# A batch-conditioned linear layer on one core: ring bursts in pairs, one part of the weights loaded twice, and other load times

## The chip, the cores and the metric

The kernel runs on one core of one Trainium2 chip. Its time is device time in microseconds, the median of several executions; the profile is of one execution.

## The reference

```python
masked_w = weight * mask[None, :, :]                 # (8, 512, 512)
w_bot = jnp.einsum('bg,got->bot', y, masked_w)       # y: (128, 8), one 512x512 matrix per batch row
return x + (jnp.einsum('bnt,bot->bno', x, w_bot) + bias)   # x: (128, 128, 512), fp32
```

So each of 128 batch rows has its own matrix, a mix of eight masked ones, and the kernel adds an identity to it so that x itself comes out of the same product.

## The kernel before

**Units, groups, steps.** The work is cut into 16 units: 4 blocks of 32 batch rows times 4 slices of 128 outputs. A unit has 8 groups of 4 batch rows. A step n (0 to 127) is one group: `group(n)` (L529) makes 16 fp32 products of 128x128 (32 passes in the trace, L543) into one of two PSUM banks; VectorE adds the bias (`add_bias`, L458), ScalarE issues the store of the output (`store_out`, L392). Its matrices lie in the buffer `wbot`, which holds one unit.

**Bursts.** The matrices of a unit are made while the unit before is used, in 8 bursts of 4 chunks; a chunk fills one of six PSUM banks (`ps1`). Bursts 0 to 15 are fp32 products (`first_burst`, L506), evicted by VectorE (L445) and completed with an identity by GpSimd (`add_one`, L357). From burst 16 on (`burst`, L524) a chunk is 8 bf16 products of 98 rows by 64 columns, evicted by ScalarE (`evict`, L387) into `wbot`. Chunk k of burst c takes the place of batch row 4c + k of the unit that was used last, so its eviction waits until group c has come to that batch row (`chunk_ready`). `bursts_before(n)` says which bursts TensorE makes ahead of group n: one each step, burst n + 8. A chunk also waits for room, that is for the eviction of the chunk six before it (`room`).

**The ring.** A burst's stationary rows stand in one of six slots: 6 blocks of 16 rows (the mask times weights in three bf16 parts, part 1 three times, part 2 twice, part 3 once) and two rows of an identity. SyncE loads parts 1 and 2 (32 rows, 256 KB), part 3 (128 KB) and the identity rows (16 KB); VectorE copies within the slot, 32 rows (`duplicate`, L436) and 16 rows (L437). A load waits until the burst six before has been made, and until the parts that it reads have been stored.

**The parts.** Each weight is read and used from its three parts. They are made in 32 tiles: load (`raw`, L242), mask multiply on VectorE (L430), first part by a cast on ScalarE (L378), remainder on GpSimd (L348), second part on ScalarE (L382), third on GpSimd (L350), store to `w_parts` in memory (`store_parts`, L255), which are then loaded again for each unit. `TILES_AT` says at which step a tile is made: 0 to 3 during the first bursts, 4 to 15 in steps 0 to 7, from step 8 on two tiles in three steps, the last at step 30.

**The order.** All is written out by hand. SyncE issues every load and the parts' stores, in the order of its program: at step n the stores of the tiles of step n - 2, a load of raw weights, ring loads (`load_burst`), and a load of x (`load_x`, L284, 1 MB, one of 8 slots) where `X_AT` says so. It waits in that order too. x is read four times 8 loads, each load used by one group of four units; the loads of the second 8 go out at steps 25, 26, 28, 29, 31, 33, 34, 36, for use from step 32 to 39.

## Time and profile before

| | us |
|---|---|
| median of 3 runs | 663.26 (662.29 to 663.32) |
| the profiled execution | 660.4 |
| its span, first to last instruction | 658.6 |
| TensorE busy (matmul) | 633.7, 96% |
| VectorE busy | 452.4, 69% |
| ScalarE busy | 312.3, 47% |
| GpSimd busy | 123.2, 19% |
| DMA | 141.30 MB, mean 215 GB/s |

The span and what lies around it make the 660.4 us. A share is an average over the span: GpSimd works only in the first third, with the tiles, and DMA is at its busiest there.

### The profile page before, as it was taken

To read this page: it belongs to the slowest core of one execution; us is meant where nothing else is said; L and a number is where in the kernel's file an instruction comes from. 1 tells how busy PE (TensorE), PEld (TensorE's weight loads), DVE (VectorE), ACT (ScalarE), POOL (GpSimd) and SP (SyncE) were. 2 spreads that over 40 slices of the span, in tenths; PEclk is the share of its full clock that TensorE was granted. 3 is DMA by queue.
4 is the path that set the end of the run, shared out by engine and by line. 5 is a ranking of instruction groups with operands and counts; after the bars stand their busy time and mean duration, and the time that the engine had idled before them with its cause. 6 is when DMAs were issued, how large, how long until landed. Compare 5 with 4: busy or idle time off the path is not lost.

```text
span 658.6 us, 18464 instructions
## 1 busy us (share of the span) xinstructions
PE 633.7 (96%) x7808; PEld 598.7 (91%) x7808; DVE 452.4 (69%) x449; ACT 312.3 (47%) x513; POOL 123.2 (19%) x95
## 2 busy tenths in 40 slices
PE   6989979999999997999999999999999999999998
PEld 2467759999999997999999999999999999999997
DVE  4976769889999763767666676766767667676521
ACT  0132216666666553555555555555555555555500
POOL 5685746445555000000000000000000000000000
PEclk9999999999999997999999999999999999999999
DMA  8979939889889995565569986555579995553122
GB/s 321 388 228 311 370 80 289 244 229 246 238 266 335 272 304 161 144 161 140 150 206 278 282 291 198 150 141 159 137 214 284 280 314 158 159 146 99 53 78 80
DMA packets 62881, 141.30 MB, mean 215 GB/s; under 512 B 7694, under 2 KB 33392, under 8 KB 52976
## 3 DMA queue, kind: packets, MB, share of 16 engines
q1 hardware_dynamic: 43856, 106.19, 54.5%
q10 hardware_dynamic: 18944, 33.93, 16.1%
q8 instruction: 62, 1.02, 0.6%
q14 instruction: 19, 0.16, 0.1%
HBM read 93.96 MB, written 46.14 MB: 213 GB/s over the span
## 4 chain that ended last, share of the span: by engine, by line
PE 81%; DVE 10%; DMA 3%; issue 3%; POOL 2%; ACT 0%; SPq 0%; DVEq 0%; ACTq 0%
PE ps L543 61%; PE ps L524 13%; PE ps L506 7%; DVE ring L437 5%; DVE ring L436 3%; DMA xs<-in_x 3%; DVE staged L458 1%; DVE raw L430 1%; POOL wbot L357 1%; DMA first_sb<-in_first 1%; POOL raw L348 1%; POOL parts L350 0%; DVE yblk L464 0%; ACT parts L378 0%; ACT wbot L387 0%
## 5 line engine op out<-in xcount | busy, mean ns | idle before, releaser
L543 PE MATMUL ps<-wbot,xs 128*128 128x128 f32 x4096 | 489.9, 278 | 7.8 <-DMA xs<-in_x 5.6
L543 PEld LDWEIGHTS ps<-wbot,xs 128*128 128x128 f32 x4096 | 471.1, 193 | 12.3 <-issue 6.4
L387 ACT ACTIVATE wbot<-ps 128x512 f32<-128x512 f32 x448 | 275.0, 614 | 237.6 <-PE ps L543 237.0
L458 DVE TENSOR_TENSOR staged<-ps,bias_sb 128x512 f32<-128x512 f32 x128 | 88.4, 691 | 176.9 <-PE ps L543 176.6
L437 DVE COPY ring<-ring 16x4096 bf16<-16x4096 bf16 x112 | 151.0, 1348 | 3.5
L436 DVE COPY ring<-ring 32x4096 bf16<-32x4096 bf16 x112 | 136.4, 1218 | 3.5
L524 PE MATMUL ps<-ydiag,ring 98*128 98x64 bf16 x3584 | 123.1, 193 | 8.2 <-DVE ring L437 8.2
L524 PEld LDWEIGHTS ps<-ydiag,ring 98*128 98x128 bf16 x3584 | 119.8, 98 | 10.9 <-issue 9.7
L348 POOL TENSOR_TENSOR raw<-raw,parts 128x512 f32<-128x512 f32 x32 | 49.3, 1540 | 70.4 <-ACT parts L378 70.4
L445 DVE TENSOR_TENSOR wbot<-ps,ring 128x512 f32<-128x512 f32 x64 | 43.4, 688 | 14.4 <-PE ps L506 10.0
L350 POOL TENSOR_TENSOR parts<-raw 128x512 bf16<-128x512 f32 x32 | 48.8, 1524 | 2.5
L378 ACT ACTIVATE parts<-raw 128x512 bf16<-128x512 f32 x32 | 19.9, 624 | 56.6 <-DVE raw L430 44.3
L430 DVE TENSOR_TENSOR raw<-raw,mask_sb 128x512 f32<-128x512 f32 x32 | 34.5, 1087 | 0.5
L506 PE MATMUL ps<-yblk,xs 128*128 128x512 f32 x64 | 29.2, 618 | 5.6 <-DVE yblk L464 5.6
L506 PEld LDWEIGHTS ps<-yblk,xs 128*128 128x128 f32 x64 | 12.7, 200 | 21.3 <-issue 15.0
L506 PE MATMUL ps<-yblk,ring 128*128 128x512 f32 x64 | 28.6, 592 | 0.0
L382 ACT ACTIVATE parts<-raw 128x512 bf16<-128x512 bf16 x32 | 19.9, 622 | 17.9 <-POOL raw L348 10.2
L506 PEld LDWEIGHTS ps<-yblk,ring 128*128 128x128 f32 x64 | 11.6, 190 | 12.0 <-issue 12.0
L357 POOL TENSOR_TENSOR wbot<-wbot,first_sb 128x512 f32<-128x512 f32 x16 | 20.2, 1266 | 11.1 <-DVE wbot L445 11.0
L464 DVE TENSOR_TENSOR yblk<-first_sb 128x512 f32<-128x512 f32 x1 | 0.7, 693 | 4.9 <-DMA first_sb<-in_first 4.9
L378 ACT ACT_TABLE_LOAD x1 | 1.3, 1283 | 2.7 <-issue 2.7
L338 POOL TENSOR_SCALAR staged<-staged,pick_sb 98x128 bf16<-98x128 bf16 x3 | 1.8, 602 | 0.3
(10 smaller groups left out, 4.0 us busy)
## 6 DMA issues: line engine op xcount, KB each, us to landing
xs<-in_x SPq DMA_DIRECT2D x32, 1024.0 KB, 10.0
out<-staged ACTq DMA_DIRECT2D x128, 256.0 KB, 3.3
ring<-w_parts SPq DMA_DIRECT2D x112, 256.0 KB, 4.0
ring<-w_parts SPq DMA_DIRECT2D x112, 128.0 KB, 4.3
w_parts<-parts SPq DMA_DIRECT2D x32, 384.0 KB, 5.9
raw<-in_w SPq DMA_DIRECT2D x16, 512.0 KB, 8.8
ring<-in_w SPq DMA_DIRECT2D x4, 512.0 KB, 15.2
ring<-in_eye SPq DMA_DIRECT2D x112, 16.0 KB
```

The costliest lines, as they stand in the source:

```text
L348: eng.tensor_tensor(at, at, w1, ALU.subtract).then_inc(s_rest, 1)
L350: eng.tensor_tensor(parts[:, t % PARTN, 2, :, :], at, high_half(t), ALU.subtract).then_inc(s_p3, 1)
L357: eng.tensor_tensor(at, at, ident_sb[:, c * CO:(c + 1) * CO].unsqueeze(1).to_broadcast([P, W, CO]), ALU.add).then_inc(s_diag, 1)
L387: eng.activation(chunk_place(b, k), chunk_sums(b, k), ACT.Copy).then_inc(s_ev_a, 1)
L430: eng.tensor_tensor(at, at, mask_sb[:, h % 2, :].unsqueeze(1).to_broadcast([P, TG, TW]), ALU.mult).then_inc(s_mul, 1)
L436: eng.tensor_copy(ring[2 * ROWS:4 * ROWS, i, :], ring[0:2 * ROWS, i, :]).then_inc(s_dup, 1)
L437: eng.tensor_copy(ring[4 * ROWS:5 * ROWS, i, :], ring[0:ROWS, i, :]).then_inc(s_dup, 1)
L445: eng.tensor_tensor(at, ps1[(b * KT + k) % S1B][:, :].rearrange("p (b o) -> p b o", o=CO), mask_t_sb[:, k, o:o + CO].unsqueeze(1).to_broad ...
L458: eng.tensor_tensor(staged[:, n % OUTB, :].rearrange("p (b o) -> p b o", b=GB), ps2[n % S2B][:, :].rearrange("p (b o) -> p b o", b=GB), bi ...
L506: ins = eng.matmul(ps1[(b * KT + k) % S1B][:, :], raw01_sb[u][:, c, k * P:(k + 1) * P], yblk[:, :], start=True, stop=True)
L524: ins = eng.matmul(ps1[at % S1B][:, g * W * OJ:(g + 1) * W * OJ], ring[0:KALL, i, k * CW + g * P:k * CW + (g + 1) * P], ydiag[:, first:fir ...
L543: ins = eng.matmul(ps2[n % S2B][:, b * SL:(b + 1) * SL], xs[:, load % GROUPS * GB + b, k, :], at, start=(k == 0), stop=(k == KT - 1))
```

## The change

Five parts. (1) `bursts_before`: from step 8 on, bursts are made before groups 0, 2, 4, 6 and 7 of a unit: one, two, two, two, one. (2) The slots' order is another, the first three ring loads go out at step 2, burst 16's copy is made at step 6, and the other copies one step ahead as before, from step 8 on. (3) Bursts 16 to 39 load part 1 a second time (16 rows, 128 KB, with a semaphore of its own), and VectorE copies only the 32 rows. (4) Tiles from 16 on come at seven steps for five, x at ten steps for eight loads; in a step SyncE's stores stand behind its loads, and a ring load goes out only if the tiles that it reads were made three steps ago. (5) At the start GpSimd's subtractions of tiles 0 and 1 stand behind the identity additions 4 and 5, those of 2 and 3 behind all eight.

```diff
-            **{8 + (t - 16) * 3 // 2: (t,) for t in range(16, TILES)}}
+            **{8 + (t - 16) * 7 // 5: (t,) for t in range(16, TILES)}}
 def bursts_before(n):
     if n < GROUPS:
         return ((), (8,), (9,), (10,), (11,), (12,), (13,), (14, 15))[n]
-    return (n + GROUPS,) if n + GROUPS < BURSTS else ()
+    if n + GROUPS >= BURSTS or n % GROUPS in (1, 3, 5):
+        return ()
+    return (n + GROUPS,) if n % GROUPS in (0, GROUPS - 1) else (n + GROUPS - 1, n + GROUPS)
-X_AT = {_g: LAST_USE[_g - _g % GROUPS - GROUPS] + 1 + _g % GROUPS * 8 // 5 for _g in range(GROUPS, XLOADS)}
+X_AT = {_g: LAST_USE[_g - _g % GROUPS - GROUPS] + 1 + _g % GROUPS * 9 // 7 for _g in range(GROUPS, XLOADS)}
 def slot_of(b):
-    return (b - FB + 4) % RING
+    return (4, 5, 0, 2, 3, 1)[(b - FB) % RING]
+def thrice(b):
+    return b < FB + 3 * CS
 def free_before(b):
     r = b - FB
     if r < 3:
         return 0
+    if r == RING - 1:
+        return GROUPS
...
+COPIES = [0] * (FB + 1)
+for _b in range(FB, BURSTS):
+    COPIES.append(COPIES[-1] + (1 if thrice(_b) else 2))
 SyncE, load_burst
-                elif b >= FB + 4:
+                elif b >= FB + 5:
+                    eng.wait_ge(s_ev_v, FB * KT)
+                elif b >= FB + 3:
                     eng.wait_ge(s_s1, FB * KT)
-                elif b >= FB + 3:
-                    eng.wait_ge(s_ev_v, FB * KT)
...
+                if thrice(b):
+                    w1 = scratch[h, 0, :, :, c % KT * BW:(c % KT + 1) * BW].rearrange("g o c -> (g o) c")
+                    eng.dma_start(ring[4 * ROWS:5 * ROWS, i, :], w1).then_inc(s_w1[i], 16)
 SyncE, the steps
-            kept = EARLY
+            kept = 0
             for n in range(STEPS):
-                for t in TILES_AT.get(n - 2, ()):
-                    store_parts(t)
-                    kept = t + 1
+                kept = max((kept, EARLY if n >= 2 else 0, *(t + 1 for t in TILES_AT.get(n - 3, ()))))
...
                 for g in range(GROUPS, XLOADS):
                     if X_AT[g] == n:
                         load_x(g)
+                for t in TILES_AT.get(n - 2, ()):
+                    store_parts(t)
 GpSimd
             for c in range(CS):
                 add_one(c)
-                if c >= CS - EARLY:
-                    subtract(c - CS + EARLY)
+                if c in (4, 5):
+                    subtract(c - 4)
+            subtract(2)
+            subtract(3)
 VectorE
-                eng.tensor_copy(ring[4 * ROWS:5 * ROWS, i, :], ring[0:ROWS, i, :]).then_inc(s_dup, 1)
+                if not thrice(b):
+                    eng.tensor_copy(ring[4 * ROWS:5 * ROWS, i, :], ring[0:ROWS, i, :]).then_inc(s_dup, 1)
...
-                while made < BURSTS and made <= LAST_BURST[min(n + 1 + AHEAD, STEPS)]:
+                if n == GROUPS - 2:
+                    duplicate(FB)
+                    made += 1
+                while n >= GROUPS and made < BURSTS and made <= n + GROUPS + AHEAD:
                     duplicate(made)
                     made += 1
 TensorE, burst
+                if thrice(b):
+                    eng.wait_ge(s_w1[i], 16 * (turn + 1))
                 eng.wait_ge(s_eye[i], 16 * (turn + 1))
-                eng.wait_ge(s_dup, 2 * (b - FB + 1))
+                eng.wait_ge(s_dup, COPIES[b + 1])
```

TensorE's program from group 8 to group 10, before; a row `ps_k<-ydiag,ring` is one chunk of a burst and its PSUM bank, a row `<-wbot,xs` a group:

```order
L543 MATMUL ps_0<-wbot,xs 128x128 x16
L524 MATMUL ps_2<-ydiag,ring 128x64 x8
L524 MATMUL ps_3<-ydiag,ring 128x64 x8
L524 MATMUL ps_4<-ydiag,ring 128x64 x8
L524 MATMUL ps_5<-ydiag,ring 128x64 x8
L543 MATMUL ps_1<-wbot,xs 128x128 x16
L524 MATMUL ps_0<-ydiag,ring 128x64 x8
L524 MATMUL ps_1<-ydiag,ring 128x64 x8
L524 MATMUL ps_2<-ydiag,ring 128x64 x8
L524 MATMUL ps_3<-ydiag,ring 128x64 x8
L543 MATMUL ps_0<-wbot,xs 128x128 x16
```

The same place after:

```order
L568 MATMUL ps_0<-wbot,xs 128x128 x16
L568 MATMUL ps_1<-wbot,xs 128x128 x16
L549 MATMUL ps_2<-ydiag,ring 128x64 x8
L549 MATMUL ps_3<-ydiag,ring 128x64 x8
L549 MATMUL ps_4<-ydiag,ring 128x64 x8
L549 MATMUL ps_5<-ydiag,ring 128x64 x8
L549 MATMUL ps_0<-ydiag,ring 128x64 x8
L549 MATMUL ps_1<-ydiag,ring 128x64 x8
L549 MATMUL ps_2<-ydiag,ring 128x64 x8
L549 MATMUL ps_3<-ydiag,ring 128x64 x8
L568 MATMUL ps_0<-wbot,xs 128x128 x16
```

Bursts 17 and 18 stand in a row, and their last two chunks use the banks of their first two.

VectorE's program at steps 7 and 8, before: evictions of burst 15 (`wbot<-ps`), the ring copies of burst 16, a mask multiply, a bias add (`staged<-ps`):

```order
L445 TENSOR_TENSOR wbot<-ps_0,ring 128x512
L445 TENSOR_TENSOR wbot<-ps_1,ring 128x512
L445 TENSOR_TENSOR wbot<-ps_2,ring 128x512
L445 TENSOR_TENSOR wbot<-ps_3,ring 128x512
L436 COPY ring<-ring 32x4096
L437 COPY ring<-ring 16x4096
L430 TENSOR_TENSOR raw<-raw,mask_sb 128x512
L458 TENSOR_TENSOR staged<-ps_1,bias_sb 128x512
```

After, from the copy of burst 16 on:

```order
L455 COPY ring<-ring 32x4096
L449 TENSOR_TENSOR raw<-raw,mask_sb 128x512 x2
L478 TENSOR_TENSOR staged<-ps_0,bias_sb 128x512
L465 TENSOR_TENSOR wbot<-ps_2,ring 128x512
L465 TENSOR_TENSOR wbot<-ps_3,ring 128x512
L465 TENSOR_TENSOR wbot<-ps_4,ring 128x512
L465 TENSOR_TENSOR wbot<-ps_5,ring 128x512
L465 TENSOR_TENSOR wbot<-ps_0,ring 128x512
L465 TENSOR_TENSOR wbot<-ps_1,ring 128x512
L465 TENSOR_TENSOR wbot<-ps_2,ring 128x512
L465 TENSOR_TENSOR wbot<-ps_3,ring 128x512
L449 TENSOR_TENSOR raw<-raw,mask_sb 128x512
```

The copy of burst 16, now one of 32 rows alone, has moved ahead of the eight evictions of step 7.

SyncE's program at steps 29 to 32, before, with the semaphores that a row waits for (`s_store` tells that a tile's parts are in memory, `s_s2` that groups are done, `s_s1` that bursts are made):

```order
L284 DMA xs<-in_x 128x2048 [waits s_s2]
L255 DMA w_parts<-parts 128x6x256 [waits s_p3,s_p2]
L284 DMA xs<-in_x 128x2048 [waits s_s2]
L255 DMA w_parts<-parts 128x6x256 [waits s_p3,s_p2]
L272 DMA ring<-in_eye 2x2048 [waits s_store1,s_store0,s_s1,s_store4,s_store3]
L275 DMA ring<-w_parts 32x4096
L276 DMA ring<-w_parts 16x4096
```

After, steps 28 to 32:

```order
L301 DMA xs<-in_x 128x2048 [waits s_s2]
L269 DMA w_parts<-parts 128x6x256 [waits s_p3,s_p2] x2
L286 DMA ring<-in_eye 2x2048 [waits s_store2,s_store1,s_s1,s_store0,s_store4]
L289 DMA ring<-w_parts 32x4096
L290 DMA ring<-w_parts 16x4096
L301 DMA xs<-in_x 128x2048 [waits s_s2] x2
L269 DMA w_parts<-parts 128x6x256 [waits s_p3,s_p2]
L286 DMA ring<-in_eye 2x2048 [waits s_store1,s_store0,s_s1,s_store4,s_store3]
L289 DMA ring<-w_parts 32x4096
L290 DMA ring<-w_parts 16x4096
```

The loads of x come one to two steps sooner by then, and the ring load that waits for the last tiles still stands behind the last store.

## Rows read from the trace of the kernel before

**Rows 1.** The page: an engine's busy time; two groups (count | busy, mean ns)

```profile
PE 633.7 (96%) x7808; PEld 598.7 (91%) x7808; DVE 452.4 (69%) x449; ACT 312.3 (47%) x513; POOL 123.2 (19%) x95
...
L543 PE MATMUL ps<-wbot,xs 128*128 128x128 f32 x4096 | 489.9, 278 | 7.8 <-DMA xs<-in_x 5.6
...
L524 PE MATMUL ps<-ydiag,ring 98*128 98x64 bf16 x3584 | 123.1, 193 | 8.2 <-DVE ring L437 8.2
```

**Rows 2.** What TensorE waited for: us in total, times, longest us

```profile
PE ps L524 <- DVE ring L437: 8.2, 9, 3.5
...
PE ps L543 <- DMA xs<-in_x: 5.6, 2, 4.4
```

**Rows 3.** Windows: us, busy of PE, PEld, DVE, ACT, POOL, clock, DMA share, GB/s

```profile
194.00:220.00 26.00, 24.88 (x360) 24.51 (x360) 22.60 (x21) 16.98 (x29) 12.36 (x7) 1.00 1.04 335
...
110.00:180.00 70.00, 67.00 (x917) 66.08 (x916) 63.00 (x54) 44.98 (x77) 36.27 (x20) 1.00 0.87 243
```

**Rows 4.** The chain of waits, a steady step: start us, us, what

```profile
442.77 0.94 PE ps L524 x32
443.70 3.65 PE ps L543 x32
```

**Rows 5.** Timeline at step 8: start us, us, instruction [idle before <-releaser]

```profile
92.14 1.15 POOL L357 TENSOR_TENSOR wbot<-wbot,first_sb 128x512 f32<-128x512 f32 x1 [4.93 <-DVE wbot L445]
...
93.15 0.69 DVE L445 TENSOR_TENSOR wbot<-ps,ring 128x512 f32<-128x512 f32 x1 [0.20 <-PE ps L543]
...
96.59 1.30 PE L524 MATMUL ps<-ydiag,ring 98*128 98x64 bf16 x32 [3.55 <-DVE ring L437]
```

**Rows 6.** Windows of the groups behind the two long waits

```profile
253.30:259.24 5.94, 5.94 (x38) 5.93 (x39) 0.00 (x0) 1.81 (x3) 0.00 (x0) 0.63 0.21 79
97.70:102.95 5.25, 5.25 (x42) 5.24 (x40) 4.69 (x3) 1.86 (x4) 4.02 (x2) 0.71 1.03 239
```

**Rows 7.** Timeline of a steady step

```profile
448.13 3.82 PE L543 MATMUL ps<-wbot,xs 128*128 128x128 f32 x32
...
449.36 0.62 ACT L387 ACTIVATE wbot<-ps 128x512 f32<-128x512 f32 x1 [1.29 <-PE ps L543]
```

**Rows 8.** Timeline of a step with tiles

```profile
109.11 1.22 DVE L436 COPY ring<-ring 32x4096 bf16<-32x4096 bf16 x1
110.36 2.07 DVE L437 COPY ring<-ring 16x4096 bf16<-16x4096 bf16 x1
...
112.78 1.09 PE L524 MATMUL ps<-ydiag,ring 98*128 98x64 bf16 x32 [0.65 <-DVE ring L437]
```

**Rows 9.** What SyncE's queue waited for: us in total, times, longest

```profile
SPq L204 <- DMA w_parts<-parts: 11.4, 2, 5.8
```

**Rows 10.** DMA from 180.9 to 253.3 us

```profile
DMA packets 9297, 21.15 MB, mean 292 GB/s; under 512 B 960, under 2 KB 5568, under 8 KB 7534
```

**Rows 11.** Timeline ahead of group 0

```profile
35.01 1.60 POOL L357 TENSOR_TENSOR wbot<-wbot,first_sb 128x512 f32<-128x512 f32 x1
...
35.53 1.27 DVE L445 TENSOR_TENSOR wbot<-ps,ring 128x512 f32<-128x512 f32 x2
...
36.76 1.46 PE L543 MATMUL ps<-wbot,xs 128*128 128x128 f32 x11 [1.95 <-POOL wbot L357]
```

**Rows 12.** The chain of waits, the last unit, which has no bursts

```profile
627.02 0.14 issue
627.16 28.17 PE ps L543 x250
```

**Rows 13.** Timeline: two evictions of ScalarE in a row

```profile
483.55 1.25 ACT L387 ACTIVATE wbot<-ps 128x512 f32<-128x512 f32 x2 [0.57 <-PE ps L543]
```

**Rows 14.** Timeline: ScalarE, an eviction and a cast

```profile
132.10 0.62 ACT L387 ACTIVATE wbot<-ps 128x512 f32<-128x512 f32 x1 [0.28 <-PE ps L543]
132.61 0.62 ACT L378 ACTIVATE parts<-raw 128x512 bf16<-128x512 f32 x1
```

**Rows 15.** Timeline: GpSimd's subtraction

```profile
138.43 1.98 POOL L348 TENSOR_TENSOR raw<-raw,parts 128x512 f32<-128x512 f32 x1 [1.44 <-ACT parts L378]
```

More of the change, by code:

```diff
@@ L185, in cond_resid_kernel @@
         s_w3 = [sem(f"s_w3_{i}") for i in range(RING)]
+        s_w1 = [sem(f"s_w1_{i}") for i in range(RING)]
         s_eye = [sem(f"s_eye{i}") for i in range(RING)]
```

## The prediction

> **What bounds the kernel now.** I read the page's engine line, then the list of what TensorE waited for, then the windows, and only then the timelines of the places which those three name. TensorE is busy for 633.7 of 658.6 us [rows 1], so anything off its path counts only by the TensorE waits that it makes or ends. Those waits are few [rows 2]: 8.2 us for VectorE's copies in the ring (9 waits, the longest 3.5), 5.6 us for two loads of x, 1.9 us for GpSimd at the first group; the 5.6 us for yblk are the start and stay. The windows say where: DMA is 0.87 busy from 110 to 180 us, with the clock granted at 1.00, and saturated from 194 to 220 us (share 1.04, 335 GB/s) [rows 3]. Away from the waits a step is 0.94 us of burst plus 3.65 us of group, 4.59 us [rows 4].
>
> **Part 1, the copy ahead of the first ring burst: -5.2 us.** Before, VectorE makes burst 16's two copies behind the last eviction of unit 1, so TensorE stands for 3.55 us [rows 5]. Its clock is then granted at 0.71 over the next group, which takes 5.25 us where one at full clock takes 3.82, and the burst takes 1.30 for 1.09 [rows 5 to 8]: 1.6 us. After, the copy stands one step earlier, and slots 4, 5, 0 are loaded at step 2, long before. What is late next: VectorE's eviction ends at 93.84 us (93.15 + 0.69) and GpSimd's identity add at 93.29 (92.14 + 1.15) [rows 5]; TensorE's group ends at 93.0 (96.59 - 3.55) and the burst covers it up to 93.0 + 0.94 = 93.9. So both terms go whole: 3.55 + 1.6 = 5.2.
>
> **Part 2, part 1 of the weights loaded twice: -4.7 us.** The other eight copy waits (8.2 - 3.5) lie in the steps with tiles: VectorE copies for 1.22 us and then for 2.07 us beside GpSimd, and TensorE's group has ended 0.65 us before [rows 8]. The 16-partition copy goes for bursts 16 to 39, that is for all those steps; 2.07 (or 1.22) us less on VectorE is more than the 0.65 by which it was late, in each of the eight places. 4.7 us go. The price is 24 transfers of 128 KB. Bytes per step rise from about 1.11 MB (ring 0.41, store 0.39 and raw 0.26 at 2 tiles in 3 steps, out 0.26) to 1.3 MB (ring 0.54, tiles 5 in 7 steps), at 4.6 us 280 GB/s, against 292 over the longest saturated stretch and 335 in a shorter one [rows 3, 10]. A ring load has 3 to 5 steps (14 us and more) before its copy, so some lag is covered. I take 0; if the queue moved only 250 GB/s, it would lag by 16 steps x 0.6 = 10 us, still within the cover, and that is the other end for the ring; it would be paid at x (rival b).
>
> **Part 3, x over ten groups, loads behind their stores: -6.9 us.** Before, x costs 5.6 us of waits [rows 2], and the group behind the second runs at clock 0.63, 5.94 us for 3.82 [rows 6, 7]: 7.7 in all. Two causes show: SyncE stands twice, 11.4 us together, at a ring load which waits for a store issued just before [rows 9], and 21.15 MB had to move from 180.9 us, where the first load of x goes out, to 253.3, where the last has landed, at 292 GB/s [rows 10]. After, up to the last x load the queue holds 8 loads of x (8.4 MB), 10 ring loads (4.1) and one more w1, 5 stores (2.0), a raw load (0.5) and 13 outputs (3.4): 18.6 MB, 63.7 us at 292. It has 14 steps (25 to 39) of about 4.68 us, 65.5 us. The slack is under 2 us, and one SyncE wait remains (the load for burst 44 stands right behind the last store). I leave 0.8 us of wait as a mean: 7.7 - 0.8 = 6.9. Ends: all 7.7 gone, or all still there.
>
> The Trainium skill (DMA: Bandwidth & Descriptors, Bandwidth) gives 341 GB/s for a 1 MB transfer by itself; by that the 18.6 MB would take 55 us, no wait could remain and the sum would be 0.8 us lower. The row of 292 GB/s over 72 us, with small and large transfers mixed, decides against counting on it.
>
> **Part 4, GpSimd's order at the start: -0.8 us.** Group 0 waits until GpSimd's last identity add ends at 36.61 us [rows 11], behind two subtractions of tile 2. Without these (2.2 us) it would end near 34.4, while TensorE waits from 34.8 (36.76 - 1.95). But VectorE's last eviction ends at 36.80 (35.53 + 1.27) and group 0 needs it 0.7 us in, so only some 0.5 us is open, plus what VectorE gains with less of GpSimd beside it. Ends 0 and 1.95; I take 0.8.
>
> **Part 5, bursts in pairs: +9.6 us, and this decides the size.** What goes: a group after a burst takes 3.65 us, eight groups in a row take 28.17 us for 250 matmuls, less 0.28 of latency 3.57 for 32 [rows 1, 4, 12]. So a switch costs 0.08 us; three fewer in each of 14 units are 42 x 0.08 = 3.4 us. What comes: a pair writes eight PSUM banks and there are six, so its seventh and eighth chunks wait for the evictions of its first and second. Before, two groups' worth of time lay between. With 0.94/32 us a matmul, the first chunk's last matmul starts 0.20 us into the pair; it takes 0.19, and ScalarE starts about 0.10 later (449.36 against 448.13 + 0.08 + 7 x 0.112 + 0.28 = 449.27 in the steady step [rows 1, 7]): 0.49. Two evictions in a row take 1.25 us [rows 13]: 1.74. TensorE starts 0.14 us after a ScalarE release [rows 12]: 1.88. The eighth chunk would start at 56 matmuls, 1.64. That is 0.24 us of wait in every pair, 42 x 0.24 = 10.1 us. The seventh is free: 0.49 + 0.61 + 0.14 = 1.24 before 1.40. Bounds: ScalarE starts a cast 0.51 us behind an eviction [rows 14]; were evictions to follow each other so, the wait would be 0.13 (5.5 us in all); at the distance that a group's batches now give them, 8 x 28.17/250 = 0.90 [rows 12], it is 0.52 (21.8 us). I take the row of two evictions in a row.
>
> In the tile steps ScalarE also has casts. Behind an even step's last eviction (about 6.0 us into the pair) come two casts at 0.51; GpSimd's subtraction takes up to 1.98 us [rows 15] from 7.7 on, that tile's second cast runs at 9.6, and where the odd step has a tile too, its cast at 10.1, so the next pair's first eviction starts at 10.6 instead of 9.85. 0.16 us of that is slack: about 0.65 us for the four pairs at steps 10, 14, 18 and 28, and 0.1 for three others, 2.9 us. Ends 0 and 4.
>
> Part 5 in all: -3.4 + 10.1 + 2.9 = +9.6.
>
> **Sum.** -5.2 - 4.7 - 6.9 - 0.8 + 9.6 = -8.0 us on the profiled execution: span 658.6 to 650.6, its time 660.4 to 652.4. The median of the runs is 663.26, 2.9 above the profiled one; I forecast a median of 655.3.
>
> **Rivals.** (a) The pairs do not wait, since evictions follow at less than I think or the matmul stream is slower at the switch. For it: the wait is a small difference of two times. Against it: even at 0.51 the eighth chunk is 0.13 late. Then 655.3 - 10.1 - 2.9 = 642.3 us. (b) The x wait stays, because 128 KB more per burst and a faster pace fill the queue that is already at 1.04: 655.3 + 6.9 = 662.2 us. For it: under 2 us of slack by my own count. Against it: of SyncE's two stands one is left. (c) The slower side: ScalarE's evictions in a pair follow each other at 0.90 instead of 0.62 us. Place: the eighth chunk of each of the 42 pairs. Price 21.8 instead of 10.1: 655.3 + 11.7 = 667.0 us. It decides from a wait of (10.1 + 8.0)/42 = 0.43 us a pair on. Against it: the 1.25 us row. (d) The short waits lower the clock: each pair would then be followed by a group at 5.9 instead of 3.8 us, 42 x 2.1 = 88 us, 743 us. Against it: copy waits like the one of 0.65 us lie in the window 110 to 180, clock 1.00 [rows 3, 8]. The Trainium skill (TensorE: Matmul & The Clock Gate, A second HAM failure mode) has such a case, TensorE idling briefly between groups as it cycles through PSUM banks; this trace does not agree, with 1.00 there.
>
> **How the numbers follow.** Forecast 0.62, (a) 0.17, (b) 0.12, (c) 0.08, (d) 0.01. The forecast's own range, from its bounds (pairs 5.5 to 14, tiles 0 to 4, x up to 3), is 649 to 660. To hold 8 in 10 I reach a good part towards (a) and take in (b): 645 to 663. 0.2% (1.3 us) is what a measurement of this kernel can tell from no change, so faster means below 661.9: all of (a), nearly all of the forecast and a part of (b), 0.86; same 0.06; slower, (c) with the rest of (b), 0.08.
>
> **What would show it.** Part 1: TensorE goes from group 7 into burst 16 with no idle time and the clock stays at 1.0. Part 2: no TensorE wait on a ring copy from 100 to 215 us. Part 3: no wait on x at groups 38 and 39, SyncE waiting once for a store. Part 5: 42 new TensorE waits on ScalarE's eviction, in each pair's last chunk, 0.13 to 0.3 us each, longer in the tile steps; a unit of eight steps takes 36.5 + 0.7 = 37.2 us where it took 36.7. It would be wrong if a unit takes 36.5 us or less, if those waits are over 0.4 us, or if bursts wait for ring loads.

## The result, and the profile after

The changed kernel takes 644.84 us (median of 4 runs, 643.54 to 649.15) against 662.77 us for the kernel before (4 runs, 661.58 to 663.32): ratio 0.9743, 95% interval 0.9694 to 0.9792. On another chip it was 645.95 against 661.52, ratio 0.9755 (0.9727 to 0.9783). The forecast was 655.3 us with a range from 645 to 663; the direction was right, the gain more than twice as large (17.9 us for 8.0), and the time just outside the range. The profiled execution took 643.54 us, its span 641.1. A unit of eight steps (groups 40 to 47) takes 36.46 us where it took 36.71: at 36.5 or less the prediction had said that it would be wrong.

The page of the changed kernel, which answers to [rows 1]:

```profile
PE 629.0 (98%) x7808; PEld 594.3 (93%) x7808; DVE 411.7 (64%) x425; ACT 297.0 (46%) x513; POOL 110.2 (17%) x95
...
L568 PE MATMUL ps<-wbot,xs 128*128 128x128 f32 x4096 | 478.2, 277 | 0.8 <-DVE wbot L465 0.4
...
L549 PE MATMUL ps<-ydiag,ring 98*128 98x64 bf16 x3584 | 117.2, 193 | 2.8 <-DVE ring L457 2.5
```

TensorE does the same work; its idle time before groups fell from 7.8 to 0.8 us and before bursts from 8.2 to 2.8. What it waited for, beside [rows 2], again us in total, times, longest; the 5.2 us for yblk at the start are left out:

```profile
PE ps L549 <- DVE ring L457: 2.5, 1, 2.5
PE ps L568 <- DVE wbot L465: 0.4, 1, 0.4
PE ps L568 <- ACT wbot L406: 0.2, 1, 0.2
PE ps L568 <- POOL wbot L374: 0.2, 1, 0.2
```

All eight waits of the tile steps, the one ahead of burst 16 and both waits on x are gone. One new wait of 2.5 us has come, and there is no list of 42 waits on ScalarE. That list alone does not settle it: in the run with five banks below every pair takes 0.48 us longer, and TensorE's list there names two such waits, 0.6 us in all. What settles it is the length of a pair. The windows of [rows 3], in the changed kernel:

```profile
110.00:180.00 70.00, 69.87 (x996) 69.52 (x996) 41.32 (x41) 47.56 (x84) 29.23 (x22) 1.00 1.02 310
194.00:220.00 26.00, 26.00 (x358) 25.97 (x355) 14.65 (x15) 14.16 (x25) 2.30 (x2) 1.00 0.90 288
```

DMA is now full in the tile steps (1.02 where it was 0.87), and VectorE is busy for 41.3 of 70 us where it was for 63.0.

A steady pair in the chain of waits (start us, us, what), beside [rows 4]:

```profile
443.81 1.87 PE ps L549 x64
```

64 matmuls in 1.87 us are two bursts of 0.94 with nothing between; so are all 30 pairs from group 40 on (1.87 or 1.88). The timeline shows ScalarE beside it, an eviction 0.44 us after the pair's first matmul and the next one 0.51 later:

```profile
443.64 2.03 PE L549 MATMUL ps<-ydiag,ring 98*128 98x64 bf16 x64
...
444.08 0.62 ACT L406 ACTIVATE wbot<-ps 128x512 f32<-128x512 f32 x1 [3.13 <-PE ps L549]
...
444.59 1.58 ACT L406 ACTIVATE wbot<-ps 128x512 f32<-128x512 f32 x3
```

I cut both kernels into stretches, from the first matmul of one group to that of another (us, from the timelines; one burst of 0.94 us that stood ahead of group 9 before stands behind its start after):

| stretch | before | after | difference |
|---|---|---|---|
| start to group 1 | 43.84 | 43.71 | -0.1 |
| group 1 to 9 | 59.89 | 53.63 | -6.3 |
| group 9 to 32 | 111.47 | 106.91 | -4.6 |
| group 32 to 40 | 44.81 | 40.71 | -4.1 |
| group 40 to 120 | 366.13 | 363.73 | -2.4 |
| group 120 to the end | 32.44 | 32.44 | 0 |

The differences add up to the 17.5 us between the spans. Corrected for the moved burst, the second and third rows are -5.3 and -5.5.

The one long wait that is left, in the chain of the changed kernel:

```profile
203.77 0.44 SPq L301
...
204.31 13.15 DMA w_parts<-parts
...
217.91 3.47 DMA ring<-w_parts
...
221.40 0.04 DVE ring L455
...
222.65 1.23 DVE ring L457
...
224.13 1.09 PE ps L549 x32
```

The last store of parts is issued behind two loads of x (L301) into a busy queue (DMA 0.94 busy from 164 to 217 us) and takes 13.15 us to land. SyncE stands for it at the ring load of burst 44; that load takes 3.47 us, two copies follow, and TensorE has been idle for 2.46 us. Then the clock is granted at half for a while: groups 36 and 37 take 8.86 us together where two take 7.23. (The texts on record call this the stop at group 35; it stands between groups 35 and 36.) The window behind the stop, in the columns of [rows 3]:

```profile
225.30:228.60 3.30, 3.30 (x17) 3.30 (x17) 2.10 (x2) 1.49 (x3) 0.00 (x0) 0.50 0.99 300
```

The stop also hides something. The last load of x lands at 239.58 us, and group 39, which needs it, starts at 240.37. The stop and its clock had put that group back by 4.25 us; without them it would have been due at 236.1, and would have waited some 3.4 us for x.

### The profile page after: what moved, and what is told of

The parts are those of the page before. It is cut to its first block, busy times and chain, and to the rows that moved or that the text cites. A ratio compares the mean times of both kernels' runs of the same rounds, so it can differ in the third digit from the quotient of the medians.

```text
span 641.1 us, 18487 instructions
## 1 busy us (share of the span) xinstructions
PE 629.0 (98%) x7808; PEld 594.3 (93%) x7808; DVE 411.7 (64%) x425; ACT 297.0 (46%) x513; POOL 110.2 (17%) x95
## 3 DMA queue, kind: packets, MB, share of 16 engines
q8 instruction: 62, 1.02, 0.7%
## 4 chain that ended last, share of the span: by engine, by line
PE 93%; DMA 3%; DVE 2%; issue 1%; ACT 1%; SPq 0%; ACTq 0%; DVEq 0%
PE ps L568 70%; PE ps L549 15%; PE ps L529 7%; DMA w_parts<-parts 2%; DVE wbot L465 1%; DVE raw L449 1%; ACT wbot L406 1%; DMA first_sb<-in_first 1%; DMA ring<-w_parts 1%; DVE ring L457 0%; DVE yblk L484 0%; DVE staged L478 0%; SPq L301 0%; SPq L286 0%; DVE ring L455 0%
## 5 line engine op out<-in xcount | busy, mean ns | idle before, releaser
L568 PE MATMUL ps<-wbot,xs 128*128 128x128 f32 x4096 | 478.2, 277 | 0.8 <-DVE wbot L465 0.4
L568 PEld LDWEIGHTS ps<-wbot,xs 128*128 128x128 f32 x4096 | 466.0, 193 | 5.5 <-issue 4.7
L406 ACT ACTIVATE wbot<-ps 128x512 f32<-128x512 f32 x448 | 259.5, 610 | 224.2 <-PE ps L568 115.8
L549 PE MATMUL ps<-ydiag,ring 98*128 98x64 bf16 x3584 | 117.2, 193 | 2.8 <-DVE ring L457 2.5
L549 PEld LDWEIGHTS ps<-ydiag,ring 98*128 98x128 bf16 x3584 | 114.8, 98 | 4.3 <-issue 2.6
L457 DVE COPY ring<-ring 16x4096 bf16<-16x4096 bf16 x88 | 107.2, 1218 | 2.7
L365 POOL TENSOR_TENSOR raw<-raw,parts 128x512 f32<-128x512 f32 x32 | 45.7, 1428 | 68.9 <-ACT parts L397 68.8
L367 POOL TENSOR_TENSOR parts<-raw 128x512 bf16<-128x512 f32 x32 | 39.1, 1221 | 2.5
L449 DVE TENSOR_TENSOR raw<-raw,mask_sb 128x512 f32<-128x512 f32 x32 | 36.6, 1155 | 0.5
```

Source lines behind the costliest of these rows:

```text
L365: eng.tensor_tensor(at, at, w1, ALU.subtract).then_inc(s_rest, 1)
L367: eng.tensor_tensor(parts[:, t % PARTN, 2, :, :], at, high_half(t), ALU.subtract).then_inc(s_p3, 1)
L406: eng.activation(chunk_place(b, k), chunk_sums(b, k), ACT.Copy).then_inc(s_ev_a, 1)
L449: eng.tensor_tensor(at, at, mask_sb[:, h % 2, :].unsqueeze(1).to_broadcast([P, TG, TW]), ALU.mult).then_inc(s_mul, 1)
L457: eng.tensor_copy(ring[4 * ROWS:5 * ROWS, i, :], ring[0:ROWS, i, :]).then_inc(s_dup, 1)
L549: ins = eng.matmul(ps1[at % S1B][:, g * W * OJ:(g + 1) * W * OJ], ring[0:KALL, i, k * CW + g * P:k * CW + (g + 1) * P], ydiag[:, first:fir ...
```

## The experiments

Each set of runs has runs of the kernel before on the same chip; ratios are to those, with 95% intervals. A run that is compared with the changed kernel across two chips is compared by these ratios. Stretches are of the profiled execution, in the order group 9 to 32, 32 to 40, 40 to 120; the changed kernel has 106.91, 40.71, 363.73, the kernel before 111.47, 44.81, 366.13.

**Are the pairs free?** One burst before each group, all else as changed:

```diff
-    if n + GROUPS >= BURSTS or n % GROUPS in (1, 3, 5):
-        return ()
-    return (n + GROUPS,) if n % GROUPS in (0, GROUPS - 1) else (n + GROUPS - 1, n + GROUPS)
+    return (n + GROUPS,) if n + GROUPS < BURSTS else ()
```

> The changed kernel with one burst before each group again, all else as changed. Theory S (a pair saves three switches of 0.08 us a unit and waits for nothing outside the tile steps): from group 40 to group 120 the time goes back from 363.7 to 366.1 us, as in the kernel before, and from group 9 to 32 the 1.0 us of pair waits goes while 8 switches (0.6 us) come back; whole kernel 2 to 4 us slower than the changed one if the stop at group 35 stays alike, ratio about 1.005. Theory P (the pairs do wait, as the prediction had it, and something else in the change made up for it): one burst a step would be faster than the changed kernel by up to 10 us. The stop of 2.5 us behind the ring load of burst 44 should shrink or stay, since burst 44 is needed at step 36 in both.

Measured: 649.52 us, ratio 0.9831 (0.9800 to 0.9862); stretches 105.53, 44.98, 366.13. The last is the kernel before's to the hundredth: in 10 units, 30 pairs save 2.40 us, 0.08 us each, and wait for nothing. The first shows the copies' part without the pairs: 105.53 against the kernel before's 111.47, 5.9 us for the same 23 bursts. In the tile steps the pairs cost instead: 105.53 is 23 plain steps, and the changed kernel, less its one burst more, takes 0.4 us longer, in spite of 8 switches saved. The stop at burst 44 grew to 5.6 us, with half clock behind it; that is the greater part of the difference between the two kernels (4.3 of 6.4 us of span), and why it came out above the 2 to 4 us expected. Whether one burst a step made the stop grow is not shown; it differs between executions of one kernel too, as below.

**What is a bank short worth?** Five banks instead of six:

```diff
-S1B = 6
+S1B = 5
```

> The changed kernel with five PSUM banks for bursts instead of six, so that a pair's sixth, seventh and eighth chunk wait for the evictions of its first, second and third. With the times that the changed kernel's trace shows (first eviction starts 0.44 us into the pair, the next ones 0.51 apart, each 0.61 long, TensorE about 0.05 behind): the sixth chunk is free (1.10 before 1.17), the seventh waits 0.20 (1.61 against 1.41), the eighth 0.25 more (2.10 against 1.85): 0.45 us a pair, 42 pairs, 19 us slower than the changed kernel, about 664 us. With the prediction's constants (0.49, 0.62, 0.14 behind) it would be 0.07 + 0.40 + 0.39 = 0.86 us a pair, 36 us slower, about 681 us. If pairs are not tied to evictions at all: no change.

Measured: 661.08 us, ratio 1.0024 (0.9989 to 1.0060); stretches 111.25, 38.14, 378.07. The last is 14.34 us more over 30 pairs, 0.48 each, where the constants of the changed kernel's trace gave 0.45 and the prediction's 0.86. The middle one is shorter than the changed kernel's: the profiled execution, in which burst 44 is due 4 us later, has no stop there. A pair, in its timeline:

```profile
442.81 2.50 PE L549 MATMUL ps<-ydiag,ring 98*128 98x64 bf16 x64
...
443.25 0.61 ACT L406 ACTIVATE wbot<-ps 128x512 f32<-128x512 f32 x1 [3.13 <-PE ps L549]
...
443.76 1.58 ACT L406 ACTIVATE wbot<-ps 128x512 f32<-128x512 f32 x3
...
444.41 0.29 PEld L549 LDWEIGHTS ps<-ydiag,ring 98*128 98x128 bf16 x8 [0.15 <-ACT wbot L406]
...
444.90 0.29 PEld L549 LDWEIGHTS ps<-ydiag,ring 98*128 98x128 bf16 x8 [0.20 <-ACT wbot L406]
```

The second eviction ends near 443.76 + 0.61 = 444.37, and TensorE loads weights at 444.41: it follows a release by 0.04 us. So the mechanism of the prediction is real, and with six banks it just fails to bite.

Its weight loads' waits for ScalarE, two in each pair (us in total, times, longest), and its clock:

```profile
PEld ps L549 <- ACT wbot L406: 16.0, 83, 0.5
```

```profile
core 0: 656.5 us, clock 1.000
```

In this execution 83 waits, 0.2 us as a mean and none over 0.5, did not lower the clock once; of the other nine runs five had 0.994 to 0.997, and no trace says what lowered it there. The Trainium skill (TensorE: Matmul & The Clock Gate, A second HAM failure mode) tells of a kernel whose TensorE idles briefly and often between groups as it cycles through PSUM banks, and whose clock falls and rises with it; in this run, with two short waits in each pair, it does not fall.

**Pairs alone on the kernel before:** the edit of the first experiment the other way, and nothing else of the change.

```diff
-    return (n + GROUPS,) if n + GROUPS < BURSTS else ()
+    if n + GROUPS >= BURSTS or n % GROUPS in (1, 3, 5):
+        return ()
+    return (n + GROUPS,) if n % GROUPS in (0, GROUPS - 1) else (n + GROUPS - 1, n + GROUPS)
```

> The kernel before with bursts in pairs alone, all else as before. Theory S: outside the tile steps 3.4 us less by 42 switches. In the tile steps VectorE makes two bursts' copies in a row (2 x (1.22 + 2.07 or 1.22)) behind one bias add, and each pair waits for them: the copies of a pair, 5 to 6.6 us, stand in one step of 4.6 with the mask multiply, so its eight waits of 0.65 us stay or grow. Sum between 5 us faster and 5 us slower than before, 100 to 660 us apart: from group 40 to 120 363.7 us instead of 366.1. Theory P: 42 x 0.24 = 10 us slower there.

Measured: 748.7 us, ratio 1.1333 (1.1298 to 1.1369); stretches 152.16, 41.36, 415.89. I had not seen this: 49.8 us more than the kernel before over 30 pairs, 1.66 each as a mean; two spells of half clock, 1.6 us each, are in it. VectorE and TensorE in the steady part:

```profile
435.49 1.22 DVE L438 COPY ring<-ring 32x4096 bf16<-32x4096 bf16 x1
436.74 1.22 DVE L439 COPY ring<-ring 16x4096 bf16<-16x4096 bf16 x1
437.99 1.22 DVE L438 COPY ring<-ring 32x4096 bf16<-32x4096 bf16 x1
439.24 1.22 DVE L439 COPY ring<-ring 16x4096 bf16<-16x4096 bf16 x1
```

```profile
440.71 1.09 PE L526 MATMUL ps<-ydiag,ring 98*128 98x64 bf16 x32 [1.40 <-DVE ring L439]
```

The old rule makes both bursts' copies in the step before the pair, four in a row, and the second burst starts only when the fourth has ended at 440.46. The changed rule (`made <= n + GROUPS + AHEAD`) makes one burst's copies in each step. From group 40 on the changed kernel differs from this one in that rule, in the slots' order and in when x is loaded, and its pairs take 1.87 us where these take 3.43. That the rule is what frees them is read from the four copies in a row; no run has it alone. The prediction priced pairs without naming that line.

**Part 1 loaded once again:**

```diff
 def thrice(b):
-    return b < FB + 3 * CS
+    return False
```

> The changed kernel with part 1 loaded once for every burst again and its 16 rows copied by VectorE, all else as changed. Theory W (the second load pays for VectorE's time in the tile steps and costs queue time later): from group 9 to group 32 some 5 us come back (the kernel before lost 6.0 us there to waits on copies, of which 0.56 to 0.66 showed as idle in each of eight), less what the sparser tiles spare VectorE; the queue has 3.1 MB less to move by group 35, 10 us at 300 GB/s, so the 2.46 us stop for burst 44 goes, with its 1.6 us of clock. Net 0 to 3 us slower than the changed kernel. Theory N (the second load did nothing, the sparser tiles alone took VectorE off the path): no waits from 9 to 32, and 4 us faster.

Measured: 658.43 us, ratio 0.9946 (0.9918 to 0.9974); stretches 127.32, 36.46, 363.73. The stop at burst 44 is gone, as with 3.1 MB less in the queue it should be, but the tile steps cost 20.4 us, four times what I expected: 13.7 in their nine pairs, 6.7 in groups behind them at half clock. Timeline of the first pair's second burst:

```profile
102.99 1.42 DVE L449 TENSOR_TENSOR raw<-raw,mask_sb 128x512 f32<-128x512 f32 x1
...
103.22 0.63 PE L549 MATMUL ps<-ydiag,ring 98*128 98x64 bf16 x16 [1.90 <-DVE ring L457]
...
104.44 0.63 ACT L397 ACTIVATE parts<-raw 128x512 bf16<-128x512 f32 x1 [1.90 <-DVE raw L449]
104.98 0.59 ACT L406 ACTIVATE wbot<-ps 128x512 f32<-128x512 f32 x1
...
105.62 0.61 PE L549 MATMUL ps<-ydiag,ring 98*128 98x64 bf16 x8 [1.78 <-ACT wbot L406]
```

TensorE first waits for the 16-row copy (1.90 us). Behind that copy VectorE is late with the mask multiply, ScalarE's cast waits for it, and the pair's first eviction stands behind the cast: 1.78 us more. The clock falls too (0.987 over the span). So the second load is what lets pairs stand beside tiles.

**Who stands in front of whom in the queue?** Stores ahead of x:

```diff
-                for g in range(GROUPS, XLOADS):
-                    if X_AT[g] == n:
-                        load_x(g)
                 for t in TILES_AT.get(n - 2, ()):
                     store_parts(t)
+                for g in range(GROUPS, XLOADS):
+                    if X_AT[g] == n:
+                        load_x(g)
```

> The changed kernel with each step's stores of parts issued before its load of x (the ring loads still first). Theory F (the 2.46 us stop at group 35 and the 1.6 us of half clock behind it come from SyncE standing 12.4 us at the ring load of burst 44 until the last store lands, and that store stands behind two loads of x in the queue): the last store goes out ahead of one load of x (3 us of the queue), lands some 3 us sooner, and the ring load of burst 44 with it; the stop shrinks from 2.5 us to 0 to 0.5, the clock stays at 1.0, 3 to 4 us faster, about 641 us. Theory B (the queue as a whole is full, only bytes count): the stop moves to x at group 38 or 39 and the time is the same.

Measured: 642.99 us, ratio 0.9725 (0.9693 to 0.9757); stretches 106.91, 41.22, 363.74. Neither theory: the store landed 1.65 us sooner (215.81 instead of 217.46), but the ring load at 221.40 instead of 221.38 us, and the stop was 2.43 us. The second load of x now stood between the store and the ring load, and landed at 219.86, so the ring load took 5.15 us instead of 3.47. The time does not separate it from the changed kernel. Two of its six runs (639.65 and 639.91 us) had a clock of 1.000 and 0.999, as none of the changed kernel's ten had; without their traces it is open whether the stop was gone there.

**The last tile a step sooner as well:** the edit just above, stores ahead of x, and on top of it

```diff
-            **{8 + (t - 16) * 7 // 5: (t,) for t in range(16, TILES)}}
+            **{8 + (t - 16) * 4 // 3: (t,) for t in range(16, TILES)}}
```

> The changed kernel with each step's stores ahead of its load of x, and tiles from 16 on at four steps for three instead of seven for five, so that the last tile is made at step 28 and not 29. Theory F (burst 44's load is late because the last tile's store comes late into a full queue): the ring loads of bursts 44 to 46 go out a step sooner and ahead of two loads of x, so the stop at group 35 is gone, the clock stays, 3.5 to 4.5 us less than the changed kernel (e3_store_first alone moved the store's landing by 1.65 us and not the stop); a wait for the last load of x of 0.3 to 1 us may come at group 39. Theory B (bytes only): the stop moves to group 39 in full, no gain. Price: the tile steps are denser on ScalarE, 0 to 0.5 us.

Measured: 639.83 us (5 runs, 639.00 to 640.92), ratio 0.9671 (0.9652 to 0.9690); stretches 107.14, 36.46, 363.73. The stop is gone, x is not waited for (its last load lands at 234.89 us, group 39 starts at 235.58), and the clock was 1.000 in all runs. Its tiles are denser than even the kernel before's (four steps for three), and group 9 to 32 is only 0.2 us longer than with seven for five: so it was not the sparser tiles that ended the copy waits. On the same chip the changed kernel run again stopped for 4.2 us (stretches 106.91, 43.66, 363.73):

> The changed kernel itself, to stand beside the other three on this chip. Ratio to the kernel before 0.974 as measured, its stop at burst 44 between 0 and 5 us from run to run.

This version beats the kernel before and, by intervals that do not touch, the changed kernel on the same chip. Earlier tiles without the stores' new place were not run. SyncE still stands at a store, but for 9.4 us in one wait:

```profile
SPq L218 <- DMA w_parts<-parts: 9.4, 1, 9.4
```

**The old rule for stores and ring loads:** a step's stores first, and `kept` counting tiles of step n - 2 instead of n - 3.

```diff
-                kept = max((kept, EARLY if n >= 2 else 0, *(t + 1 for t in TILES_AT.get(n - 3, ()))))
+                for t in TILES_AT.get(n - 2, ()):
+                    store_parts(t)
+                kept = max((kept, EARLY if n >= 2 else 0, *(t + 1 for t in TILES_AT.get(n - 2, ()))))
...
-                for t in TILES_AT.get(n - 2, ()):
-                    store_parts(t)
```

> The changed kernel with the old rule for stores and ring loads (a step's stores go out first, and a ring load may stand right behind them), all else as changed. Theory G (keeping ring loads a step behind the stores is what freed SyncE): SyncE stands for 5 us and more at bursts 36 and 40 again, x goes out later, and x is waited for at groups 37 to 39, 2 to 6 us slower than the changed kernel. Theory H (what freed x is its ten steps instead of twelve and fewer stores; the rule only shifts where SyncE stands): the stop at burst 44 stays 2 to 3 us, since that load waits for the last store in either, and the time is within 1.5 us of the changed kernel.

Measured: 642.09 us (637.43 to 647.95), ratio 0.9692 (0.9649 to 0.9735); stretches 106.90, 43.06, 363.72. The profiled run waits for x (3.1 us) and for ring copies (1.2 us); three others had full clock and, at 637.43 to 639.59 us, were faster than any of the changed kernel. So the new rule gained nothing that can be seen. SyncE stands 15.4 us at stores with the old one and 18.0 with the new, and 18.7 with either if the waits for stores that the trace puts down to the ring load's own line are added.

**x over twelve steps again:**

```diff
-X_AT = {_g: LAST_USE[_g - _g % GROUPS - GROUPS] + 1 + _g % GROUPS * 9 // 7 for _g in range(GROUPS, XLOADS)}
+X_AT = {_g: LAST_USE[_g - _g % GROUPS - GROUPS] + 1 + _g % GROUPS * 8 // 5 for _g in range(GROUPS, XLOADS)}
```

> The changed kernel with x over twelve steps again. Theory Q (one full queue; who stands in front decides where TensorE stops): the ring load of burst 44 no longer stands behind two early loads of x, so the stop at group 35 shrinks by 2 us or goes, and the last loads of x, issued at steps 33, 34 and 36, are waited for at groups 37 to 39, 2 to 5 us with the clock; in sum within 2 us of the changed kernel. Theory T (ten steps are what keeps x from being late and burst 44 has nothing to do with it): the stop at 35 stays and x adds 5 us, slower by 5 us or more.

Measured: 648.69 us, ratio 0.9825 (0.9798 to 0.9852); stretches 106.88, 45.80, 363.72. No stop at burst 44, but 6.2 us of waits on x:

```profile
PE ps L568 <- DMA xs<-in_x: 6.2, 2, 3.9
```

Of theory Q the place was right, the size was not: by the ratios it is about 4.5 us slower than the changed kernel. The ten steps are worth that.

**Burst 16's copy late again:**

```diff
-                if n == GROUPS - 2:
+                if n == GROUPS - 1:
```

> The changed kernel with burst 16's copy at step 7 again, behind the evictions (one copy of 32 rows, not two). It then ends 1.25 us before the place where the two copies ended: TensorE should stand 2.3 us (3.55 - 1.25) ahead of burst 16, 0.16 more than the record shows, and the clock may fall over the next group (0 to 1.6 us). Theory C (the copy's place is worth what the prediction said): 2.4 to 4 us slower than the changed kernel. Rival: something else, such as the ring's slots or the earlier loads, took the wait away, and nothing changes.

Measured: 646.51 us (644.09 to 650.64), ratio 0.9782 (0.9745 to 0.9819). The whole time does not separate it from the changed kernel; the profiled execution is the slowest of the four. Its timeline shows what was expected:

```profile
95.11 1.57 PE L549 MATMUL ps<-ydiag,ring 98*128 98x64 bf16 x32 [2.30 <-DVE ring L455]
```

Group 1 to 9 takes 57.69 instead of 53.63 us, 4.1 more, of which 1.6 are the clock. Add the 1.25 us of the second copy, which this run does not make, and it is the 5.3 of Part 1.

**GpSimd's old order at the start:**

```diff
-                if c in (4, 5):
-                    subtract(c - 4)
-            subtract(2)
-            subtract(3)
+                if c >= CS - EARLY:
+                    subtract(c - CS + EARLY)
```

> The changed kernel with GpSimd's old order at the start. The prediction gave the new order 0.8 us (0 to 1.95). In the traces group 1 starts at 43.84 us before and at 43.71 and 43.47 after. Theory V (VectorE's evictions hold group 0, not GpSimd): group 1 starts within 0.3 us of the changed kernel's. Theory G: 0.8 us or more later.

Measured: 644.04 us, ratio 0.9730 (0.9702 to 0.9758), not to be told from the changed kernel. In the profile group 1 starts at 44.22 us, against 43.71 and 43.47, but that start also depends on how long TensorE's first matmuls run at half pace (0.85 us each, then 0.43), which differs between executions of one kernel. Counted from TensorE's twentieth matmul, when the pace is full, group 1 starts after 28.49 us here, after 28.51 in the kernel before, and after 27.74 (within 0.01) in the ten traces with GpSimd's new order and nothing else changed there. So the order is worth 0.76 us, the prediction's 0.8, and my theory V is out. Group 0 itself starts 1.8 us sooner with it, and then loses 1.0 us to VectorE's last evictions.

**VectorE's mask multiply of tile 3 behind the last evictions**, on top of e9_tiles_sooner:

```diff
-                if c >= CS - EARLY:
+                if CS - EARLY <= c < CS - 1:
...
+            multiply_mask(EARLY - 1)
```

> e9_tiles_sooner with VectorE's mask multiply of tile 3 moved behind its last two evictions of the first unit. In the changed kernel's trace the first group takes 8.10 us from start to the next one's start where 7.01 is normal, with VectorE's eviction as releaser: the last evictions stand behind a mask multiply. Theory V (that order is what holds group 0): group 0 to 1 takes 7.1 us, about 1 us less, near 638.8 us. Theory G (GpSimd or the weights' loads hold it): no change. Price: tile 3 one microsecond later, hidden.

Measured: 639.39 us (636.98 to 642.69), ratio 0.9671 (0.9645 to 0.9698). Group 0 to 1 takes 7.08 us instead of 8.10, as theory V said, and group 1 starts at 42.60. But group 8 then loses 0.43 us, where TensorE waits for GpSimd, and the profiled run waited 1.5 us for x ahead of group 39; the time is that of e9_tiles_sooner. What is gained at the start was not kept at the end; that the shift of the queue did it is argued, not shown.

## Why the prediction was wrong

**Part 5, bursts in pairs, failed: +9.6 forecast, -2.2 measured** (-2.4 us from group 40 to 120, -0.25 from 32 to 40, +0.4 in the tile steps, by the run with one burst each). The failed step is the wait of 0.24 us that each pair was given, "TensorE starts 0.14 us after a ScalarE release [rows 12]: 1.88" against "The eighth chunk would start at 56 matmuls, 1.64". Each of its terms was taken from a place that was not the pair's. ScalarE starts at 0.44 us, not 0.49. Two evictions in a row take 0.51 + 0.61 = 1.12 us, not the 1.25 of [rows 13]; there, in the trace, the second eviction starts 0.61 us behind the first and 0.10 behind the end of the group's last matmul (484.16 and 484.06 us), so it had most likely waited for that, which a merged row does not tell; and [rows 14] had the 0.51. And TensorE follows a release by 0.04 to 0.05 us in a burst, not by the 0.14 of [rows 12], where it had been at rest ahead of a group. In sum 0.44 + 1.12 + 0.05 = 1.61, before 1.64: a gap of 0.24 us became a slack of 0.03 in each pair. The bounds I gave (0.13 to 0.52) did not hold the value either, since only one of three terms was bounded. In the tile steps the waits that I worked out are there, but smaller: four pairs take 2.50, 2.27, 2.26 and 2.25 us where 2.04 is free, 1.1 us in all for the 2.9. The chain of the second:

```profile
119.75 0.48 PE ps L549 x16
...
120.29 1.12 ACT wbot L406 x2
...
121.45 0.41 PE ps L549 x8
```

The switches gave 0.08 us each, as forecast: 3.4 us in all, of which 2.40 are in the stretch from group 40 to 120. I held a rival (a) at 0.17 that had this right; its 642.3 us came within 2.5 us of the measured 644.84, and lacked the next point and the 1.1 us.

**Part 3: -6.9 forecast, -3.9 in the profiled run** (from group 32 to 40, 8.1 us over eight plain steps before, 4.25 over a pair unit's 36.46 after). x is no longer waited for, but only because the stop had put its last group back: landed at 239.58 us, it would have been 3.4 late for a group due at 236.1. The count of the queue, 18.6 MB for 65.5 us, is not to blame: e9_tiles_sooner moves the same bytes and lands that load at 234.89, since SyncE issues it at 214.37 us and not at 224.07. The count left out that SyncE, while it stands at a store, lets the queue run low. The changed kernel, as it ends:

```profile
217.00:221.00 4.00, 4.00 (x49) 3.99 (x48) 0.69 (x1) 0.61 (x1) 0.00 (x0) 1.00 0.55 153
```

What was mis-sized is the "0.8 us of wait": I named the ring load of burst 44 behind the last store, and priced it as part of the slack of x. Its store took 13 us to land, and the stop was 2.5, 4.2, 4.4 and 3.2 us in four profiled executions with that order, each with half clock behind it. SyncE stood twice at stores, 18.0 us, not once. With x over twelve steps, and with the old rule for stores, the wait shows at x instead; of the profiled executions with the changed kernel's bytes and pairs at six banks, only that of e9_tiles_sooner has neither.

**Part 2: -4.7 forecast, -5.9 measured without pairs** (111.47 against 105.53 us; -5.5 with the tile steps' pair waits inside). The eight idle times of [rows 2] add up to 4.7, but the stretch of the kernel before was 5.9 us longer than 23 steps of 4.59. A matmul's record runs 0.16 us past the start of the next in a stream (3.82 against 3.65 in [rows 4, 7]), so each recorded idle time is that much too short. And the experiment without the second load shows what I had not worked out: with pairs it is worth 20 us in the tile steps, not 5. The price of 0 for its bytes is not shown to hold: without them the stop at burst 44 is gone.

**Part 1: -5.2 forecast, -5.3 measured**, by its own steps, the clock included. The slots' new order and the ring loads at step 2 were in every run of the changed kernel; what they give by themselves is not shown. **Part 4: -0.8 forecast, -0.76 in the experiment**, hidden in the result by a start at half pace that lasted to 10.2 us instead of 8.6 and put the twentieth matmul back by 0.64.

In sum, against the forecast, the pairs were 11.8 us off one way and part 2 another 1.2; x and the ring were 3.0 off the other way, and the start 0.7. That is the 9.4 us by which the span came out below the 650.6 forecast. That the time came as near to the range as it did is luck: the misses of part 3 and of the start took back 3.7 us.

## What to carry to other kernels

A small difference of two chains of latencies that recurs 42 times is not to be priced from single rows of other places: bound every term, and if the sign of the slack is within the bounds, say so in the forecast. When a queue is full, ask of each transfer what stands ahead of it and who is waiting behind its landing; the last store of a phase, and the load that needs it, are worth more than the mean use of the queue. Edits that look separate may be each other's condition: here pairs alone made the kernel before 88 us slower, for want of the copies' new order, and the changed kernel without its second load is 12.5 us slower on the same chip.

## What the runs showed of the hardware

ScalarE starts an eviction of 128x512 from PSUM 0.51 us behind the one before, though each takes 0.61. TensorE follows its release by 0.04 us when it waits inside a stream, by 0.14 when it had been at rest ahead of a group.

A ring copy and GpSimd's subtraction did not run side by side: the one that started first went first. The kernel before, beside group 8:

```profile
97.69 1.22 DVE L436 COPY ring<-ring 32x4096 bf16<-32x4096 bf16 x1
...
97.80 2.12 POOL L348 TENSOR_TENSOR raw<-raw,parts 128x512 f32<-128x512 f32 x1 [4.51 <-ACT parts L378]
...
98.94 2.06 DVE L437 COPY ring<-ring 16x4096 bf16<-16x4096 bf16 x1
...
100.00 1.90 POOL L350 TENSOR_TENSOR parts<-raw 128x512 bf16<-128x512 f32 x1
```

The 32-row copy starts 0.11 us before the subtraction and takes its 1.22 us; the subtraction ends 1.02 us behind it, at 99.93. The 16-row copy starts while the subtraction is under way, and ends 1.08 us behind its end, at 101.01. So the 2.07 us of [rows 8] came not from the size of the copy but from its place: there too a subtraction ended 1.08 us before it (111.35 and 112.43). With nothing of GpSimd's under way the same copy took 1.22, and in the changed kernel a 32-row copy that started behind a subtraction took 1.35.

In the kernel with pairs alone TensorE waited 1.40 us in every pair, and the granted clock from 400 to 500 us was 1.00. The stops of 2.3 us and more that are told above had half clock behind them, and so had the two of 1.90 and 1.78 us, close together, in the run without the second load.

The stop of the changed kernel was 2.5 us in the execution of 643.54 us and 4.2 in that of 645.63; that it is also what makes the runs differ (643.5 to 649.2 us) is likely but not traced. e9_tiles_sooner, which has no stop, stays within 1.9 us.
